# Causal masking by 43 constant contraction rows in place of mask matmuls and GpSimd clearing, in a gated attention and expert layer on one core

## The reference, cut to what matters

```python
# per sequence, heads of 8 channels
q, k, v    = heads(LN(x) @ Wq + bq), heads(LN(x) @ Wk + bk), heads(LN(x) @ Wv + bv)
att        = where(tril(ones(T, T)), q @ k.T * 8 ** -0.5, -inf)      # "self": causal
y          = softmax(att) @ v
qc, kc, vc = heads(LN(x) @ Wcq + bcq), heads(ctx @ Wck + bck), heads(ctx @ Wcv + bcv)
y         += softmax(qc @ kc.T * 8 ** -0.5) @ vc                      # "cross": not causal
x          = x + tanh(g_xattn) * (y @ Wp + bp)
# feed-forward: router over 16 experts in 4 groups (top 2 groups, top 4 experts), all experts computed
out        = sum over e of combine[:, e] * (silu(xf @ w_gate[e].T) * (xf @ w_up[e].T)) @ w_down[e].T
x          = x + tanh(g_ffn) * out
```

## Time and profile before

| what | value |
|---|---|
| median of 3 runs | 382.51 us (382.36 to 383.38) |
| the profiled execution: its time, its span | 381.71 us, 379.9 us |
| mean granted TensorE clock | 0.991 of full |
| PE / DVE / ACT / POOL busy | 91% / 71% / 54% / 53% of the span |

### The profile page before, as it was taken

The page is one execution under the profiler, slowest core; times in us unless marked ns, Lnnn a source line. Parts: engine busy times, 40 slices in busy tenths (PEclk is TensorE's granted clock), DMA queues, the critical chain, the costliest instruction groups (busy, mean ns, idle before and its releaser), DMA issues.

```text
span 379.9 us, 8947 instructions
## 1 busy us (share of the span) xinstructions
PE 346.4 (91%) x3200; PEld 250.6 (66%) x3200; DVE 270.2 (71%) x742; ACT 206.0 (54%) x442; POOL 200.6 (53%) x304
## 2 busy tenths in 40 slices
PE   1759989999999999999999999999999989997594
PEld 0423556676777787677876788678867867865454
DVE  2127588686898789888787778777788785566751
ACT  1321247688767645676467645864576557643020
POOL 5935031564870889079525992185704830955313
PEclk9999999999999999999999999999999999999789
DMA  3265144463344742494315422644044204105060
GB/s 92 83 201 155 59 126 144 142 205 117 94 127 129 159 145 60 138 172 126 112 47 127 129 89 93 150 91 117 17 133 96 43 14 94 23 18 110 2 125 16
DMA packets 31325, 39.13 MB, mean 103 GB/s; under 512 B 2832, under 2 KB 28592, under 8 KB 28848
## 3 DMA queue, kind: packets, MB, share of 16 engines
q1 hardware_dynamic: 31280, 38.55, 37.9%
HBM read 30.89 MB, written 7.47 MB: 101 GB/s over the span
## 4 chain that ended last, share of the span: by engine, by line
PE 77%; DVE 8%; DMA 5%; SPq 3%; ACT 2%; issue 2%; POOL 2%; POOLq 0%; ACTq 0%
PE bank L737 13%; PE bank L717 12%; PE bank L704 8%; PE bank L805 7%; PE bank L806 6%; PE bank L814 6%; PE bank L701 5%; DMA k_stack<-part_scr 5%; PE bank L695 4%; PE bank L775 3%; PE bank L756 2%; PE bank L743 2%; SPq L444 2%; PE bank L758 1%; PE bank L765 1%
## 5 line engine op out<-in xcount | busy, mean ns | idle before, releaser
L859 DVE TENSOR_REDUCE row_max<-bank 128x2 f32<-128x512 f32 (+1 forms) x224 | 149.3, 686 | 46.4 <-PE bank L704 27.4
L627 ACT ACTIVATE probs<-bank 128x512 f32<-128x512 f32 x224 | 128.6, 596 | 54.7 <-PE bank L717 44.7
L717 PE MATMUL bank<-q_stack,k_stack 73*128 73x256 bf16 (+1 forms) x512 | 80.5, 259 | 0.4 <-ACT probs L627 0.3
L541 POOL TENSOR_SCALAR_AFFINE_SELECT probs<-probs 128x256 f32<-128x256 f32 (+1 forms) x96 | 44.7, 482 | 35.7 <-ACT probs L627 35.2
L737 PE MATMUL bank<-probs,v_ext 128*32 128x256 f32 (+1 forms) x1024 | 61.7, 358 | 0.0
L555 POOL TENSOR_TENSOR f_h<-f_h,comb 128x256 f32<-128x256 f32 x64 | 45.3, 725 | 22.1 <-DMA comb<-c_scr 11.3
L704 PE MATMUL bank<-k_stack,q_stack 72*128 72x256 bf16 x256 | 50.1, 290 | 5.4 <-DMA k_stack<-part_scr 4.0
L717 PEld LDWEIGHTS bank<-q_stack,k_stack 73*128 73x128 bf16 x512 | 42.3, 98 | 14.9 <-ACT probs L627 5.7
L396 POOL TENSOR_TENSOR rest<-proj,part 128x512 f32<-128x512 f32 x14 | 16.2, 1157 | 59.9 <-ACT part L604 59.9
L805 PE MATMUL bank<-xn2T,w_pairs_sb 128*128 128x256 f32 x128 | 40.7, 400 | 2.3 <-DVE f_h L946 1.4
L737 PEld LDWEIGHTS bank<-probs,v_ext 128*32 128x32 f32 x1024 | 26.7, 109 | 23.2 <-issue 8.9
(11 more groups left out here) (103 smaller groups left out, 431.0 us busy)
## 6 DMA issues: line engine op xcount, KB each, us to landing
q_stack<-part_scr SPq DMA_DIRECT2D x48, 192.0 KB
k_stack<-part_scr SPq DMA_DIRECT2D x48, 192.0 KB
comb<-c_scr SPq DMA_DIRECT2D x16, 512.0 KB, 6.9
part_scr<-part SPq DMA_DIRECT2D x48, 128.0 KB, 3.2
x_in<-in_x SPq DMA_DIRECT2D x8, 128.0 KB, 2.8
w_pairs_sb<-in_w_pairs SPq DMA_DIRECT2D x1, 1024.0 KB, 7.0
out<-y_out SPq DMA_DIRECT2D x8, 128.0 KB, 2.4
ctx_in<-in_ctxT SPq DMA_DIRECT2D x8, 64.0 KB, 3.5
```

The lines of the kernel that those rows point to most:

```text
L541: nc.gpsimd.affine_select(out=p, in_=p, compare_op=ALU.is_ge, fill=0.0, base=0, pattern=[[0, nh], [1, 128]], channel_multiplier=-1).then_i ...
L627: nc.scalar.activation(probs[:, seq % NP, :], exp_bank[s % 2][:, :], ACT.Exp).then_inc(exp_done, 1)
L717: last = pe.matmul(ps[:, n, :], k_stack[0:STACK + 1, b % SLOTS, kind, h, kt * 128:(kt + 1) * 128], q_stack[0:STACK + 1, b % SLOTS, kind, h ...
L859: nc.vector.tensor_reduce(row_max[:, kind, qt, h0:h0 + nh], max_bank[k % 2][:, :].rearrange("p (h k) -> p h k", h=nh), AX.X, ALU.max).then ...
```

## The change

The mask becomes part of the contraction. Below row 72 of the self stacks stand 43 constant rows (ROWS; three tokens to a row), so that the diagonal blocks contract over 72 + 1 + 43 = 116 rows (MASKED). In k_stack row r holds a small or large power of two at its own three tokens and 0 elsewhere; in q_stack it holds a factor of own size at its own tokens, -LATER at the tokens of lower index, and 0 at those behind. The products are of no weight where the key is allowed and about -1e31 or lower where it is not. The matmuls L695, the constants ident_b and causal, the 96 GpSimd steps L541 and the semaphore mask_done are gone.

The maxima's diagonal blocks now read row 72 as well, before the shift stands there: so every self load of q_stack has one more DMA (zero_row, 8 KB) that zeroes that row. The exponentials of a self chunk with key tile 0 go as two matmuls of 128 queries a head (116 rows on the diagonal, 73 off it) instead of one of 256. At the start GpSimd makes the rows (more), and SyncE places them (tri): into slot 0 from the small tiles, broadcast over heads, into slots 1 and 2 by copies of slot 0.

All five order lists are new. At the start: clear_values (vclear) runs before the constants (more) on GpSimd; load:1 stands ahead of the weights and load:2 ahead of the first part stores; place_constants (ones) stands between pd2:0 and pd0:0:1; qst:1 comes behind shd:0 and kst:1 instead of ahead of shd:0; tri:1 stands behind qst:1:1, tri:2 behind shd:1:1. On TensorE shift:0 follows max:0:15 instead of max:0:17, and max:1 follows exp:0:10 instead of exp:0:5.

```diff
-MASKED = -1e30
+ROW_TOKENS = 3
+ROWS = (128 + ROW_TOKENS - 1) // ROW_TOKENS
+MASKED = STACK + 1 + ROWS
+AT = (2.0 ** 40, 2.0 ** -12, 2.0 ** -64)
+FROM = (2.0 ** -70, 2.0 ** -18, 2.0 ** 34)
+LATER = 2.0 ** 92
...
+            def place_masks(s):
+                if s == 0:
+                    sp.wait_ge(const_made, 3)
+                else:
+                    sp.wait_ge(tri_in[0], 32)
+                for st, tri in ((q_stack, tri_q), (k_stack, tri_k)):
+                    first = tri[:, 0:T].unsqueeze(1).broadcast_to([ROWS, H, T])
+                    src = first if s == 0 else st[SHIFT_ROW + 1:MASKED, 0, SELF]
+                    sp.dma_start(st[SHIFT_ROW + 1:MASKED, s, SELF], src).then_inc(tri_in[s], 16)
...
+                if kind == SELF and qk == 0:
+                    if b == 0:
+                        sp.wait_ge(const_step, 4)
+                    sp.dma_start(q_stack[SHIFT_ROW:SHIFT_ROW + 1, b % SLOTS, SELF], zero_row[:, :]).then_inc(stack_in[b % SLOTS][SELF], 16)
...
             def more_constants():
                 nc.gpsimd.memset(ones_row[:, :], 1.0).then_inc(const_step, 1)
-                nc.gpsimd.memset(ident_b[:, :], 0.0).then_inc(const_step, 1)
-                nc.gpsimd.memset(causal[:, :, :], 0.0).then_inc(const_step, 1)
...
+                nc.gpsimd.memset(zero_row[:, :], 0.0).then_inc(const_step, 1)
+                at_q, at_k = (a[:, 128:].rearrange("p (r c) -> p r c", c=ROW_TOKENS) for a in (tri_q, tri_k))
+                for c in range(ROW_TOKENS):
+                    nc.gpsimd.memset(at_q[:, :, c:c + 1], -AT[c]).then_inc(const_step, 1)
+                    nc.gpsimd.memset(at_k[:, :, c:c + 1], FROM[c]).then_inc(const_step, 1)
...
-            def mask(b, m):
-                s = CROSS_C2 + m
-                _, kt, h0, nh, q0 = S2_CHUNKS[s]
-                pool.wait_ge(exp_done, b * NC2 + s + 1)
...
-                if b == 0 and k == CROSS_C1:
-                    pe.wait_ge(const_made, 3)
+                if b < SLOTS and k == CROSS_C1:
+                    pe.wait_ge(tri_in[b], 32)
...
-                if kind == SELF:
-                    pe.matmul(ps[:, :, keys - 128:keys], ident_b[:, :], causal[:, 0:nh, :], start=True, stop=False)
                 for n in range(nh):
...
+                    q, key = q_stack[:, s, kind, h0 + n, qt * 128:(qt + 1) * 128], k_stack[:, s, kind, h0 + n, :]
                     if kind == SELF:
...
+                        for kt in range(qt + 1):
+                            rows_used = MASKED if kt == qt else STACK
+                            last = pe.matmul(ps[:, n, kt * 128:(kt + 1) * 128], q[0:rows_used], key[0:rows_used, kt * 128:(kt + 1) * 128],
+                                             start=n == 0 and kt == 0, stop=n == nh - 1 and kt == qt)
...
-                    last = pe.matmul(ps[:, n, :], k_stack[0:STACK + 1, b % SLOTS, kind, h, kt * 128:(kt + 1) * 128],
-                                     q_stack[0:STACK + 1, b % SLOTS, kind, h, q0:T], start=n == 0, stop=n == nh - 1)
+                    key, q = k_stack[:, b % SLOTS, kind, h, kt * 128:(kt + 1) * 128], q_stack[:, b % SLOTS, kind, h, :]
+                    if kind == SELF:
+                        for qt in range(kt, NQ):
+                            rows_used = MASKED if kt == qt else STACK + 1
+                            last = pe.matmul(ps[:, n, qt * 128 - q0:(qt + 1) * 128 - q0], key[0:rows_used], q[0:rows_used, qt * 128:(qt + 1) * 128],
+                                             start=n == 0 and qt == kt, stop=n == nh - 1 and qt == NQ - 1)
+                    else:
+                        last = pe.matmul(ps[:, n, :], key[0:STACK + 1], q[0:STACK + 1], start=n == 0, stop=n == nh - 1)
...
-                if kind == SELF:
-                    pe.wait_ge(mask_done, b * SELF_C2 + 3 * g4 + 3)
```

More of the change, by code:

```diff
@@ L66 @@
 LAST_OF_KIND2 = (CROSS_C2, NC2)
+STACK_DMAS = (2 * PARTS, 2 * PARTS + 1)
 GU_USES = NB + 1
@@ L73 @@
     'pe': '''
[L74 to L93, removed]
@@ L230 @@
[L230 to L239 removed]
+        xnT_e:2 proj_e:2 proj_e:2:1 sh_e:0 part0:2:1 exp_e:0 exp_e:0:1 exp_e:0:2 exp_e:0:3 exp_e:0:4 exp_e:0:5
@@ new lines @@
+    'sp': '''
+        load:0 load:1 w:0 load:2 pd0:0 pd1:0 pd2:0 ones:0 pd0:0:1 qst:0 kst:0 pd1:0:1 pd2:0:1 pd1:1 tri:0 qst:0:1
+        kst:0:1 pd2:1 pd0:1 pd0:1:1 pd1:1:1 shd:0 pd2:1:1 kst:1 qst:1 kst:1:1 load:3 shd:0:1 qst:1:1 tri:0:1 pd0:2
+        load:4 pd1:2 pd2:2 pd0:2:1 shd:1 pd1:2:1 pd2:2:1 kst:2 qst:2 qst:2:1 experts:0 shd:1:1 tri:0:2 kst:2:1 pd0:3
+        pd1:3 pd2:3 shd:2 pd0:3:1 pd1:3:1 qst:3 pd2:3:1 kst:3 qst:3:1 kst:3:1 shd:2:1 cout:0 load:5 cin:0 pd0:4 pd1:4
+        pd2:4 shd:3 pd0:4:1 qst:4 kst:4 pd1:4:1 pd2:4:1 load:6 kst:4:1 shd:3:1 qst:4:1 cout:1 cin:1 pd0:5 shd:4 pd1:5
+        pd2:5 st:0 qst:5 kst:5 pd1:5:1 pd0:5:1 pd2:5:1 load:7 qst:5:1 kst:5:1 shd:4:1 pd0:6 cout:2 st:1 pd1:6 pd2:6
+        cin:2 shd:5 qst:6 pd1:6:1 kst:6 pd2:6:1 pd0:6:1 kst:6:1 shd:5:1 qst:6:1 pd0:7 cout:3 cin:3 pd1:7 shd:6 pd2:7
+        st:2 pd0:7:1 kst:7 qst:7 pd1:7:1 pd2:7:1 shd:6:1 kst:7:1 qst:7:1 cout:4 shd:7 st:3 cin:4 shd:7:1 st:4 cout:5
+        cin:5 st:5 cout:6 cin:6 cout:7 cin:7 st:6 st:7''',
@@ L343, in build @@
         const_step, const_made = sem("const_step"), sem("const_made")
+        tri_step, tri_in = sem("tri_step"), [sem(f"tri_in{s}") for s in range(SLOTS)]
         v_clear_step, v_cleared = sem("v_clear_step"), sem("v_cleared")
@@ L472, in _ @@
                     place_constants()
+                elif what == "tri":
+                    place_masks(n)
                 elif what == "experts":
@@ L490, in _ @@
             sp.wait_ge(ones_in, 16 * SLOTS)
+            for s in range(SLOTS):
+                sp.wait_ge(tri_in[s], 32)
         @block.gpsimd
@@ L573, in _ @@
                     split_step(nc.gpsimd, b, n, 2)
-                elif what == "mask":
-                    mask(b, n)
                 elif what == "yadd":
@@ L693, in max_chunk @@
                 ps = max_bank[k % 2][:, :].rearrange("p (h k) -> p h k", h=nh)
[L694 to L695 removed]
                 for n in range(nh):
[L697 to L698 removed]
+                    q, key = q_stack[:, s, kind, h0 + n, qt * 128:(qt + 1) * 128], k_stack[:, s, kind, h0 + n, :]
                     if kind == SELF:
[L700 to L702 removed]
+                        for kt in range(qt + 1):
+                            rows_used = MASKED if kt == qt else STACK
+                            last = pe.matmul(ps[:, n, kt * 128:(kt + 1) * 128], q[0:rows_used], key[0:rows_used, kt * 128:(kt + 1) * 128],
+                                             start=n == 0 and kt == 0, stop=n == nh - 1 and kt == qt)
                     else:
[L704 removed]
+                        last = pe.matmul(ps[:, n, :], q[0:STACK], key[0:STACK], start=n == 0, stop=n == nh - 1)
                 last.then_inc(max_scores, 1)
```

319 lines of the change are left out of this document (159 added, 160 removed).

## The result

The changed kernel is slower: 448.26 us (median; 446.46 to 450.21) against 382.53 us, a ratio of 1.171 (95% interval 1.166 to 1.177). Predicted were 371.9 us. The profiled execution took 450.21 us, its span 448.5 us. The kernel before scattered more in these sets than the 0.3% assumed ahead: from 380.6 to 385.2 us, with medians of 382.2 to 382.6.

The account below looks back on a forecast made before the run. TensorE's matmul issue was taken to bound the kernel from 68 to 320 us. Against 381.71 us, -12.6 + 0.2 + 0.3 + 1.5 = -10.6 gave 371.1, plus 0.8 to the median: 371.9 us; range for 8 in 10, 366.5 to 378.

Parts of the forecast that it names:

- The step that failed: Mask-row DMAs at the start, 2.1 MB at 197 GB/s: taken as zero, between 0 and 10.7 us.
- Mask matmuls removed: On TensorE, 84 of 96 mask matmuls stand in the full stretch from 68 to 320 us; removal gains 12.6 us.
- The first 12: Mask matmuls before 54 us, hidden behind VectorE's 0.68 us a chunk: counted at nothing, 1.8 us more gain if uncovered.
- Rows of contraction: Diagonal blocks on TensorE at 116 rows instead of 72 or 73: zero cost, 0.055 us per 128 columns.
- The rival of 45 us: Diagonal blocks pay a weight load not taken ahead, 0.10 us for each of 448 matmuls: 417 us, 6% chance.
- Exponentials split: Two TensorE matmuls of 128 columns for one of 256, 112 more in sequences 1 to 7: 0.2 us cost.
- GpSimd's clearing: Removing 44.7 us of GpSimd work, nobody's last wait in the full stretch: no gain, bound 0.9 us.
- SyncE and the start: Constant rows issued ahead of the load that ends the first wait: 0.3 us later, bounds 0 and 0.8.
- Waiting for VectorE: In the full stretch some freed TensorE time turns to waiting for VectorE: 1.5 us, bounds 0 and 6.3.
- a takeover: Rival: VectorE takes over, freed TensorE time turns into waits for maxima; 376.7 us, 15% chance.
- The lists: New order lists as such: no cost, within 3 us both ways; the old ones left 1.4 us idle in 252.
- the start pays: Rival: mask rows and late qst:1 hold up sequences 1 and 2; a third of 10.7, 375.5 us, 12% chance.

Follow-up runs that it names:

- plain maxima: The kernel before without the mask matmuls of its maxima, which are taken over all keys; GpSimd's clearing kept: 376.37 us (0.987), again 374.53 us (0.977).
- 48 rows: The changed kernel with 48 mask rows placed instead of 43, diagonal blocks contracting over 121 rows: 378.14 us (0.987), again 378.82 us (0.990).

## Why the prediction was wrong

- **The step that failed** is that of the mask rows: "At the 197 GB/s of 20 to 30 us that is 10.7 us of DMA ... I take zero, between 0 and 10.7 us". The bytes were right, and the bounds held nothing: the rate of the earlier trace rows is that of other DMAs. 43 rows travel on one engine at 22 GB/s, 15.2 us or more each and six of them, and whatever SyncE issues behind them waits. It cost 448.3 - 378.8 = 69.5 us of the 76.4 us by which the prediction was wrong. I had weighed how much the DMAs carry, and never how they are spread, though the count 43 stood in the diff. The prediction's own sign of being wrong, a k_stack landing as a wait of TensorE before 80 us, came true (23.6 us, ending at 70.0).
- **Mask matmuls removed, 12.6 us.** What they held was sized rightly: 11.3 us for the 77 behind 75.2 us and 1.2 for the seven before. What became of it was not: alone they gave 5.8 and 8.0 us (376.4 and 374.5 against 382.2 and 382.6 in the same sets). In the middle a third stayed behind with the clearing, and the first 75 us gave nothing, while the opening became 12 us longer. The first 12 "I count at nothing"; that the opening would change with them I had not looked at.
- **Rows of contraction, 0.** Right: about 0.055 us each at 116 rows, under 1.6 us in all at 121. The rival of 45 us falls, and the wording by which a weight load would be exposed with it. **Exponentials split, 0.2.** No gap stands at L738; not measured alone.
- **GpSimd's clearing, 0 (bound 0.9).** Mis-sized: 2.5 us alone. In the traces sequence 6's last exponential ends at nearly the same time (301.2 against 301.3 us), the last of all at 335.5 against 336.9, and 0.8 us more come behind it. Beside the plain maxima the medians differ by 1.0 us (374.5 against 373.5), inside both intervals: what the middle gains there, the first 75 us lose. "Nobody's last wait there" was read from a stretch in which TensorE was full; with fewer columns on TensorE the traces speak against it, though the wait that carries the clearing was not found.
- **SyncE and the start, 0.3.** The first cross maximum comes at 30.1 us instead of 28.5 with 48 rows, and at 29.9 us without their DMAs: 1.4 us that are the order's or the new constants', where 0.3 was taken.
- **Waiting for VectorE, 1.5.** From 68 to 320 us TensorE was busy for 248.60 of 252 us with 48 rows against 250.59, 2.0 us more idle; its rival, a takeover, did not come: VectorE is at 81%.
- **The lists, 0 within 3 us.** Mis-sized: 5 us lost where no DMAs are to be hidden, 3 to 5 us won over the old order where six of them are. The rival "the start pays" named the right place, but for the wrong reason, a shared rate, and at 3.6 us where the stalls took 66.8.
- **From the forecast to the 48-row kernel**: 371.9 us were forecast; with nothing done for causality the old order measures 373.5, the new one 378.4, and with the 48 rows 378.8. So the work left out gave 9.0 us of the 10.6 forecast, but partly by luck: the masks gave less than their share and the clearing, priced at nothing, made up for some of it. The 5 us of the order are what carries the kernel to the edge of the range. In the traced executions they are not in the opening (56.8 against 64.0 us) but between the exponentials' ends (254.5 against 250.9 us), less 1.5 us won behind them; what in the lists costs them stays open.
- A small misreading: the earlier trace rows has TensorE at eight tenths in the sixth and the thirty-third slice, not at nine; nothing rests on it.

## What to carry to other kernels

For each DMA that a change adds, factor the outer dimension of both sides before its bytes are priced: a count that is a prime above 16 is one engine. 43 rows cost 15.2 us where 42, 44 or 48 cost 4.5 or 4.6, and a padding to 48 took the stalls away. A slow DMA on a shared queue is paid by what stands behind it. And read the distances between TensorE's starts from the first microsecond: a half pace can stand there that the clock's column does not show, and here it lasted 12 us longer in the kernel without mask matmuls. Price the removal of work from an engine that is nobody's last wait again for the kernel in which the full engine has less to do. And try first the part of a change that only leaves work out, since it beat the whole here (374.5 us).

## What the runs showed of the hardware

- One DMA engine moved 20 to 24 GB/s (the changed kernel, the kernel before with 43-row DMAs, the DMAs alone), and SyncE stood still in the issues behind it, 16.21 and 17.51 us for issues that otherwise take 0.65 and 2.0 to 2.5 us.
- TensorE's pace over the first 46 to 85 us is 1.2 GHz with 1.00 in the clock's column, and its end moves between executions of one kernel (56.9 and 63.3 us).
- After TensorE's holes of 21 and 22 us in the changed kernel the column does show 0.50, and the full pace was back at 126.7 and 181.0 us, with work from 120.3 and 174.9 us on.
